# A two-layer adaLN block: float32 in place of split fp32r matmuls in the second attention and the last feed forward

## The reference

```python
q, k, v = shape(h @ Wq), shape(h @ Wk), shape(h @ Wv)      # (B, 16, 1024, 64)
weights = softmax(einsum('bhqd,bhkd->bhqk', q, k) + position_bias)
return (weights @ v) @ Wo
...
inter = h @ wi.T + bi + (h @ lora_A[e].T) @ lora_B[e].T    # for each expert e
out += gate[e] * (relu(inter) @ wo.T + bo)
```

## Time and profile before

| | us |
|---|---|
| median of 3 runs | 1040.41 (1040.23 to 1041.82) |
| the profiled execution, its time | 1039.06 |
| its span | 1037.3 |
| TensorE matmul busy | 934.1 (90%) |
| VectorE busy | 668.4 (64%) |
| ScalarE busy | 590.0 (57%) |
| GpSimd busy | 281.7 (27%) |

### The profile page before, as it was taken

How to read it: one execution, slowest core, us unless ns; L and a number is a source line. 1 busy time by engine, 2 the same in 40 slices (tenths; PEclk the granted TensorE clock), 3 DMA queues, 4 the chain that set the end, 5 groups by cost and what they waited for, 6 DMA issues and landing times. The chain is left out here.

```text
span 1037.3 us, 24542 instructions
## 1 busy us (share of the span) xinstructions
PE 934.1 (90%) x9958; PEld 687.5 (66%) x9958; DVE 668.4 (64%) x1352; ACT 590.0 (57%) x980; POOL 281.7 (27%) x332
## 2 busy tenths in 40 slices
PE   7888349457999999999999999999999999996897
PEld 6467338345777777677777767777777776774786
DVE  6277401285767777677677777667777776774665
ACT  2533113236666766766766676676667667672343
POOL 1100540332341422324233142333414233112300
PEclk9999769767999999999999999999999999999999
DMA  8301231100002002000200200110020010000000
GB/s 260 109 1 73 94 89 31 56 23 1 2 2 85 2 2 86 2 2 2 85 3 1 86 2 2 42 46 3 2 85 2 2 37 3 1 3 2 1 21 21
DMA packets 27124, 35.43 MB, mean 34 GB/s; under 512 B 6042, under 2 KB 21716, under 8 KB 26836
## 3 DMA queue, kind: packets, MB, share of 16 engines
q1 hardware_dynamic: 25988, 31.76, 9.2%
q0 software_dynamic: 1024, 2.10, 0.7%
HBM read 28.48 MB, written 5.37 MB: 33 GB/s over the span
## 5 line engine op out<-in xcount | busy, mean ns | idle before, releaser
L516 DVE CUSTOM_DVE_ANT_0 soft<-SC,strips 128x1024 f32<-128x1024 f32 x256 | 303.2, 1221 | 21.1 <-PE SC L372 21.1
L482 ACT ACTIVATE soft<-soft,nmax 128x1024 f32<-128x1024 f32 x256 | 294.0, 1149 | 2.8 <-DVE nmax L516 2.8
L524 DVE COPY PTs<-PT 128x1024 f32<-128x1024 f32 x128 | 156.8, 1225 | 186.0 <-PE PT L390 186.0
L474 ACT COPY PTs<-PT 128x1024 f32<-128x1024 f32 x128 | 129.8, 1014 | 223.9 <-PE PT L390 223.9
L406 PE MATMUL CX<-PTs,V 128*64 128x256 f32 x2048 | 250.7, 387 | 5.7 <-DVE wo_out L533 4.3
L372 PE MATMUL SC<-qk 64*128 64x512 f32 x1536 | 212.4, 409 | 10.4 <-DVE nmax L516 7.0
L390 PEld LDWEIGHTS PT<-ident,soft 64*128 64x128 f32 x4096 | 155.6, 139 | 86.5 <-issue 75.6
L406 PEld LDWEIGHTS CX<-PTs,V 128*64 128x64 f32 x2048 | 136.7, 137 | 89.7 <-issue 24.6
L390 PE MATMUL PT<-ident,soft 64*128 64x64 f32 x4096 | 180.1, 228 | 3.7 <-DVE PTs L524 2.4
L372 PEld LDWEIGHTS SC<-qk 64*128 64x128 f32 x1536 | 137.1, 188 | 35.5 <-issue 4.7
L557 POOL TENSOR_TENSOR x<-x,wo_out 128x256 f32<-128x256 f32 x64 | 47.1, 736 | 259.3 <-DVE wo_out L533 259.3
(11 more groups left out here) (235 smaller groups left out, 1041.4 us busy)
## 6 DMA issues: line engine op xcount, KB each, us to landing
strips<-bias_vec SPq DMA_DIRECT2D x8, 1920.0 KB, 7.1
arena<-in_L_ffn_w SPq DMA_DIRECT2D x1, 2048.0 KB, 10.4
slots_in<-arena SPq DMA_DIRECT2D x1, 1536.0 KB, 9.1
arena<-slots_in SPq DMA_DIRECT2D x8, 192.0 KB, 3.9
slots_out<-arena SPq DMA_DIRECT2D x8, 192.0 KB, 2.0
x<-in_L_attn_x SPq DMA_DIRECT2D x2, 512.0 KB, 4.6
out<-x SPq DMA_DIRECT2D x4, 256.0 KB, 2.3
arena<-in_L_wmod SPq DMA_DIRECT2D x2, 384.0 KB, 5.6
```

Of the source, the lines that this page charges most:

```text
L474: act.copy(turned_out(n, 0), turned_in(0)).then_inc(ev("ptA_out"), 1)
L482: act.activation(soft[:, n % RING, hd, :], soft[:, n % RING, hd, :], ACT.Exp, bias=nmax[:, j:j + 1], scale=-1.0, accum_out=rsum[:, hd, n % ...
L516: dve.tensor_tensor_reduce(soft[:, n % RING, hd, :], SC[hd][:, :], strips[:, u // B % 2, hd, i * P:i * P + S], 1.0, 3.4e38, ALU.add, ALU.m ...
L524: dve.tensor_copy(turned_out(n, 1), turned_in(1)).then_inc(ev("ptB_out"), 1)
```

## The change

The types F32R, the tensors `h_high`, `h_low`, `w_parts`, `wsplit`, `raw_qk` and the two further parts of `qk` go. q, k, h and the weights stay F32, and each group of three F32R matmuls becomes one F32 matmul. GpSimd keeps only the additions into x in the loop, VectorE and ScalarE lose their splits, and ScalarE writes q and k directly. The second `qk` buffer now lies in the free half of `probsT`. VectorE handles slot -1 (the bias of tile 1) ahead of the normalisation of batch 1's rows, before behind it.

```diff
-            act.mul(raw_qk[:, c % 2, :], chunk_bank(u, c), sign).then_inc(ev("high_out"), 1)
+            act.mul(qk[u % 2][:, "qk".index(kind), q * CK:(q + 1) * CK], chunk_bank(u, c),
+                    -1.0 if kind == "q" else 1.0).then_inc(ev("chunk_out"), 1)
...
-                for n, (hp, wp) in enumerate(((0, 0), (1, 0), (0, 1))):
-                    rhs = h_parts[hp][:, b * S + q * CK:b * S + (q + 1) * CK]
-                    if kind == "q":
-                        rhs = bass.AP(h_parts[hp], b * S + S - 1 - q * CK, [[N, P], [-1, CK]])
-                    ins = pe.matmul(bank, wsplit[:, p % 2, wp, "qk".index(kind), :], rhs, start=(n == 0), stop=(n == 2))
+                rhs = hT[:, b * S + q * CK:b * S + (q + 1) * CK]
+                if kind == "q":
+                    rhs = bass.AP(hT, b * S + S - 1 - q * CK, [[N, P], [-1, CK]])
+                ins = pe.matmul(bank, wpair[:, p % 2, "qk".index(kind), :], rhs, start=True, stop=True)
...
-                for m, (qp, kp) in enumerate(((0, 2), (0, 3), (1, 2))):
-                    for hd in range(2):
-                        mine = slice(hd * DK, hd * DK + DK)
-                        ins = pe.matmul(SC[hd][:, k * CK:(k + 1) * CK], qk[u % 2][mine, qp, i * P:(i + 1) * P],
-                                        qk[u % 2][mine, kp, k * CK:(k + 1) * CK], start=(m == 0), stop=(m == 2))
+                for hd in range(2):
+                    mine = slice(hd * DK, hd * DK + DK)
+                    ins = pe.matmul(SC[hd][:, k * CK:(k + 1) * CK], qk[u % 2][mine, 0, i * P:(i + 1) * P],
+                                    qk[u % 2][mine, 1, k * CK:(k + 1) * CK], start=True, stop=True)
...
-            what, a, c = middle(n)
-            if what == "chunk":
-                pool_chunk(pool, a, c)
-            if n % (B * TB) == 4 and n // (B * TB) + 1 < PAIRS:
-                pool_split(pool, n // (B * TB) + 1)
...
-            for k in range(2, 4):
-                pool.wait_ge(ev("h_high"), k + 1)
-                at = slice(reversed_block(k) * 512, (reversed_block(k) + 1) * 512)
-                pool.tensor_tensor(h_low[:, at], hT[:, at], h_high[:, at].bitcast(F32), ALU.subtract).then_inc(ev("h_split"), 1)
...
-            split_h(0)
             quarter_rows(1)
-            for c in range(2):
-                dve_chunk(dve, 0, c)
             gathered(2)
-            split_h(1)
-            for c in range(3, 5):
-                dve_chunk(dve, 0, c)
             gathered(3)
             norm_variance(2, 1)
             dve_slot(dve, -2)
+            dve_slot(dve, -1)
             norm_rows(2, (1,))
-            for n in range(-1, TILES + 4):
+            for n in range(TILES + 4):
...
-                    for n, (wp, hp) in enumerate(passes):
-                        mm(four_sc[c], w_parts[:, 0, wp, c * P:(c + 1) * P], h_ffn[hp][:, k * 512:(k + 1) * 512],
-                           start=(n == 0), stop=False, skip_group_check=True)
+                    mm(four_sc[c], wT[:, WI + c, :], hT[:, k * 512:(k + 1) * 512], start=True, stop=False, skip_group_check=True)
...
-                        for m, (wp, hp) in enumerate(passes):
-                            ins = mm(four_sc[c], w_parts[:, 1, wp, c * P:(c + 1) * P], masked[:, j, hp, :],
-                                     start=False, stop=(m == 2), skip_group_check=True)
-                        ins.then_inc(ev("inter_full"), 1)
+                        mm(four_sc[c], wT[:, LB + c, :], masked[:, j, :], start=False, stop=True,
+                           skip_group_check=True).then_inc(ev("inter_full"), 1)
```

More of the change, by code:

```diff
@@ L98, in build @@
         ctxs = sb("ctxs", [P, 4, 2 * P])
-        w_parts = sb("w_parts", [P, 2, 2, CK], F32R)
+        wo_out = sb("wo_out", [P, 2, 2, 2, D])
         hT = sb("hT", [P, N])
@@ L107, in build @@
         probs = sb("probs", [P, 2, S])
[L108 to L114, removed]
+        qk0 = sb("qk0", [P, 2, S])
+        probsT = sb("probsT", [P, 2, 2, TB, P])
+        qk1 = probsT[:, 1, :, :, :].rearrange("p h k q -> p h (k q)")
+        qk = (qk0[:, :, :], qk1)
         V1 = sb("V1", [P, 2, TB, P])
         wpair = sb("wpair", [P, 2, 3, P])
-        wsplit = sb("wsplit", [P, 2, 2, 2, P], F32R)
         strips = sb("strips", [P, 2, 2, STRIP])
@@ L155, in build @@
         gbb = part(flat, 27 * P, E)
[L156 to L160, removed]
+        lowrank = qk0[:, 0, 0:512]
+        masked = qk0[:, 1, :].rearrange("p (j n) -> p j n", j=2)
         hot_wide = part(flat, 0, 8 * P).rearrange("p (j t d) -> p j t d", j=2, t=4)
@@ L288, in act_chunk @@
                     act.wait_ge(ev("pv_done"), 4 * (u - 1))
[L289 removed]
+                act.copy(V1[:, u % 2, 4 * q:4 * q + 4, :].rearrange("p t d -> p (t d)"), chunk_bank(u, c)).then_inc(ev("chunk_out"), 1)
                 return
[L291 to L297, removed]
[L298 to L325 removed]
+            if u >= 2:
+                act.wait_ge(ev("scores"), 2 * TB * (u - 1))
+            act.mul(qk[u % 2][:, "qk".index(kind), q * CK:(q + 1) * CK], chunk_bank(u, c),
+                    -1.0 if kind == "q" else 1.0).then_inc(ev("chunk_out"), 1)
         def pe_chunk(pe, u, c):
@@ L331, in pe_chunk @@
             if c == 0 and b == 0:
-                pe.wait_ge(ev("w_split"), p + 1)
+                pe.wait_ge(ev("ld_pair"), 48 * p + 48)
+            if c == 0 and u == 1:
+                pe.wait_ge(ev("hT_ready"), 12)
             bank = chunk_bank(u, c)
@@ L336, in pe_chunk @@
                 if c >= 4:
[L337 removed]
+                    pe.wait_ge(ev("chunk_out"), c - 3)
             else:
                 n = (u - 1) * TB + slots_of(u)[c]
[L340 to L342 removed]
+                pe.wait_ge(ev("chunk_out"), 6 * u + c)
                 if n >= 5:
@@ L833, in _ @@
                     act.wait_ge(ev("masked"), 2 * k)
-                act.copy(lowrank[0], MI[:, :]).then_inc(ev("low_ready"), 1)
+                act.copy(lowrank, MI[:, :]).then_inc(ev("low_ready"), 1)
                 for j in range(2):
@@ L1103, in _ @@
                 dve.wait_ge(ev("low_ready"), k + 1)
-                tt(lowrank[1], MI[:, :], lowrank[0].bitcast(F32), ALU.subtract).then_inc(ev("low_split"), 1)
-                dve.wait_ge(ev("low_split"), k + 1)
                 for j in range(2):
@@ L1109, in _ @@
                         dve.wait_ge(ev("inter_full"), 8 * k)
-                    tt(masked[:, j, 0, :], PT[j][:, :], lowrank[0].bitcast(F32), ALU.mult)
-                    tt(masked[:, j, 1, :], PT[j][:, :], lowrank[1].bitcast(F32), ALU.mult).then_inc(ev("masked"), 1)
+                    tt(masked[:, j, :], PT[j][:, :], lowrank, ALU.mult).then_inc(ev("masked"), 1)
                 if k + 1 < 4:
```

78 lines of the change are left out of this document (14 added, 64 removed).

## The result

The change makes the kernel slower: 1068.39 us (median of 4 runs, 1067.26 to 1074.27) against 1040.32 (4 runs), ratio 1.0279 with a 95% interval of 1.0240 to 1.0318. That is +28.1; forecast was +33.7 and 1074, with 1065 to 1089 as the range. The profiled execution took 1068.98, its span is 1067.3, 30.0 more than before.

The account below looks back on a forecast made before the run. TensorE's matmuls were taken to bound the kernel. Scores 20.1 + 4.6, chunks 9.6, entry -5.0, feed forward 6.5 and normalisation -2.1 gave +33.7 on 1039.06; with 1.35 for the median, 1074 us, range 1065 to 1089.

Parts of the forecast that it names:

- The price: TensorE matmuls of 512 columns: one F32 product takes 0.86 us against 0.69 for the three F32R ones it replaces.
- the rival of 993: Faster rival: an F32 product costs one record's time, 0.43 us in place of 0.69, giving 993 us; chance 0.03.
- the count of passes in the prediction: Skill page on precision: true float32 takes four passes through the array, so four against three for F32R.
- Scores: Attention loop, 128 tiles: +0.31 us in 64 tiles behind an output projection (20.1), +0.07 in the others (4.6).
- The rival with 0.09 behind each of 128 groups: Slower rival: F32 scores delay the transposes behind them by about 0.09, 12 us more, 1086; chance 0.17.
- Chunks: The 60 q and k projection chunks in the loop: 1.06 us each against 0.90, +9.6 us.
- 9.1 less 4.1 is 5.0: Entry: waits of 9.1 us mostly go, dearer matmuls cost 4.1; taken as -5, bounds -8 and 0.
- the three waits: Entry: TensorE's waits of 2.84 and 2.92 us for VectorE's low part of h and 3.33 for GpSimd's, 9.1 in all.
- at a granted clock of 0.70 on average ... 4.1 at the lower level: Entry: four chunks and four tiles' scores cost 2.0 us more at full clock, 4.1 at 1.2 GHz.
- is not counted twice: Entry: VectorE's sums and tile 1's bias coming earlier is a condition for the waits to go, with no separate gain.
- Normalisation and last feed forward: After the loop: normalisation -2.1 us as GpSimd's splits go; feed forward +6.5, with steps 2 to 4 at +1.99 each.
- the entry gives more: Rival: all of the 9.1 and more goes at full clock, and tiles with VectorE's wait come out even; 1066, chance 0.05.

Follow-up runs that it names:

- run with scores alone: Kernel before, with only the scores of units 1 to 15 in plain F32: 1067.3 us against 1039.65, ratio 1.0268.
- the run with the entry alone: Kernel before, with only the change's entry: early projections and scores in F32 without splits, VectorE's new order; 1028.43 us against 1039.65, ratio 0.9892.
- the warm run: Kernel before, plus 80 unread matmuls in TensorE's waits at the entry to keep the granted clock up: 1037.7 us against 1040.15, ratio 0.9976.
- the run with three operations: Kernel with only the change's entry, plus three waiting operations on VectorE whose results nobody reads: 1033.89 us; kernel before 1039.37, ratio 0.9949.
- the run with early splits: Kernel before, with GpSimd's splits of the last feed forward's weights moved to the loop's last tile: 1037.36 us against 1040.15, ratio 0.9971.

## Why the prediction was right or wrong

**The price, right.** An F32 product against three F32R ones was forecast as 0.86 against 0.69. Pairs of score records start 0.429 apart in the changed kernel (1.72 for four pairs), and a step of the feed forward got 1.97 longer, not 1.99. Of two readings of the footnote in "Perfetto Trace Analysis" (Engine Utilization) of the Trainium skill, the one record by record is the one that holds; the rival of 993 is out. By the count of passes in the prediction, four against three, it would be a third dearer; measured is a quarter (0.86 against 0.69).

**Scores, right in mechanism and low in size.** Forecast 0.31 and 0.07 in alternate tiles, 24.7 in all (by these figures it is 64 x 0.31 and 64 x 0.07, 24.3; and the scores of tiles 0 to 3 are priced a second time at the entry). The trace gives 0.33 (607.11 to 609.33 is 2.22, before 1.89) and 0.10 (1.78 and 0.59 against 1.63 and 0.64). The run with scores alone has 120 of the 128 tiles in float32, for which the forecast comes to 23.2, and its loop gives 26.7; a unit got 1.81 longer where 1.54 was forecast. Part of what was missed is the start of the group: of projection and scores together, 2.22 less 1.72 and 0.43 leaves 0.07, as before the change, where I had let it shrink to 0.05. The rest is in the other tiles, 0.03 in the scores with the transposes behind them and about 0.02 in the transposes ahead (600.71 to 601.26 in the changed kernel against 605.12 to 605.65). The rival with 0.09 behind each of 128 groups was wrong in its place: transposes behind the scores start 1.72 after them with no such surcharge.

**Chunks, right.** 0.16 forecast, 0.165 measured; 9.6 and 9.7.

**The loop as a whole.** 34.3 forecast, 35.9 measured, and TensorE without a wait in it. That it came so near is in part luck: a unit got 2.44 longer where 2.15 was forecast, but the first tile of the stretch, from tile 3's to tile 4's scores, got 1.0 shorter (5.50 at a granted clock of 0.62 before, 4.54 at 1.00 now), for which the forecast had no term. GpSimd's work there went from 210.5 to 87.2 us and that was worth nothing, as said.

**The entry, wrong in size.** The step was "9.1 less 4.1 is 5.0", with bounds of -8 and 0; -12.7 was measured in the profile, and the run with the entry alone has a median 11.2 lower, both outside them. Term by term, from the four stretches: the three waits gave 7.3 of the 9.1, since `hT` is still waited for twice, 0.87 each. The matmuls, charged at +4.1, came to -2.8, 1.0 in the third stretch and 1.8 in the fourth. And 2.7 came from a wait that has no term. Against the forecast that is 1.8 less, 6.9 more and 2.7 more, which makes up the 7.7 to within 0.1.

So two things failed. First, "at a granted clock of 0.70 on average ... 4.1 at the lower level": I charged the new matmuls at the clock of a kernel that waits, when the waits were just what I was taking out. From tile 0's to tile 3's scores the clock was granted in full. This is the larger error. A full clock with the waits left in place gives only 1.5 back there (the warm run); the two go together, as the run with three operations shows from the other side. Second, "is not counted twice": I took VectorE's queue as a condition for the three waits to go. It is a term of its own. Tile 1's scores waited 4.52 us for tile 0's bias, which stood behind splits that waited for ScalarE, and this wait is in none of the earlier trace rows; now it is 1.47. Three such operations put back cost 4.4 us. The order of tile 1's bias, 0.9 by the stretch that it bounds, is in the same class.

**Normalisation and last feed forward, right.** -2.1 forecast, -1.9 measured between the last scores and the feed forward, outside the scatter between executions with the same splits (above); the row operations themselves went from 4.12 to 2.14, and the run with early splits shows it apart from all else. +6.5 forecast, +6.7 and +6.8 measured.

**The sum.** Against +33.7, the profiled executions differ by +30.0: 7.7 less at the entry, 1.6 more in the loop, 0.5 more behind it, and 1.9 more ahead of the change, where two executions differ anyway. That the difference of the profiled executions came within 4 of the forecast owes something to errors of opposite sign. The rival "the entry gives more", 1066 at a chance of 0.05, came nearest in mechanism at the entry, and I had it too low; its other condition, that the tiles with VectorE's wait come out even, did not hold (0.10).

## What to carry to other kernels

Price a change of type record by record, start to start, from rows of the same form in the same trace; done so, terms of 43 us in all came out 2 off, though a score price 15% low and a first tile that got faster cancelled in part. Where an engine works through its queue in order, an operation for which nobody waits delays all behind it: list each wait on that queue, not only the waits that end at the engine that bounds. And do not carry the granted clock of a stretch that waits over to the version in which it doesn't; take both levels as bounds, and ask what the waiting stretch gets back.

## What the runs showed of the hardware

GpSimd beside VectorE: `TENSOR_SCALAR` on 128x128 took 4.12 for eight beside GpSimd's splits and 2.14 without, and a `TENSOR_TENSOR` on 128x8 took 0.68 to 0.72 beside a subtraction of GpSimd's and 0.17 without. The timeline of both engines before, batch 1, shows how:

```profile
960.66 1.29 POOL L718 TENSOR_TENSOR w_parts<-strips,w_parts 128x512 fp32r<-128x512 f32 x1
961.01 0.20 DVE L884 RECIPROCAL st<-st 128x8 f32<-128x8 f32 x1 [0.34 <-ACT st L741]
961.25 0.72 DVE L885 TENSOR_TENSOR st<-st 128x8 f32<-128x8 f32 x1
961.91 0.60 POOL L723 CAST qk<-hT 128x512 fp32r<-128x512 f32 x1
962.01 0.52 DVE L886 TENSOR_TENSOR st<-st 128x8 f32<-128x8 f32 x1
```

VectorE's operation is not slowed, it is held: it ends at 961.97, when GpSimd's ends (961.95), and the next at 962.53, with GpSimd's cast (962.51). The first three of the eight `TENSOR_SCALAR` end likewise, at 963.95, 964.50 and 965.84, within 0.1 us of the three operations of GpSimd beside them, and the five behind these take 0.34 each. The `RECIPROCAL` beside the same subtraction is not held, 0.20 as without. "GPSIMD Engine Reference" (Specifications) of the Trainium skill says that GpSimd shares its SBUF interfaces with VectorE, with contention for VectorE's instructions in a 2-port mode or with two SBUF inputs; the rows of `TENSOR_TENSOR` and `RECIPROCAL` agree, and for `TENSOR_SCALAR` no run shows in which mode it was.

The joint of two groups on TensorE, read record by record at the place of the earlier trace rows and after: the first scores start 0.03 us behind the output projection's last records when they are F32R, and 0.11 when they are F32. That is why the projection seems longer in the changed kernel (0.50 against 0.42). The joint costs the same: F32R's first pair then takes 0.32 where the following take 0.23, F32's takes 0.43 like the rest, so that either way it is 0.11 to 0.12 over one pair from the projection's last start to the second pair of scores.
